# A signal for each tile and another order of TensorE's products in the edge phases of a four-layer graph network kernel

## Time and profile before

| what | value |
|---|---|
| median of 3 runs | 2502.88 us (2497.65 to 2503.34) |
| the profiled execution's own time | 2481.36 us |
| its span | 2479.6 us |
| mean granted clock of TensorE | 0.76 of full speed |
| first edge phase | about 284 to 945 us of the span |
| second edge phase | about 1568 to 2270 us of the span |

### The profile page before, as it was taken

How to read it: one execution, slowest core, us unless ns; L and a number is a source line. 1 busy time by engine, 2 the same in 40 slices (tenths; PEclk the granted TensorE clock), 3 DMA queues, 4 the chain that set the end, 5 groups by cost and what they waited for, 6 DMA issues and landing times. The chain is left out here.

```text
span 2479.6 us, 40282 instructions
## 1 busy us (share of the span) xinstructions
PE 1639.9 (66%) x9301; PEld 1175.0 (47%) x9301; DVE 1690.6 (68%) x4231; ACT 1080.0 (44%) x2994; POOL 1264.8 (51%) x1217
## 2 busy tenths in 40 slices
PE   0678466565666665289999956466676666766378
PEld 0576244343444444289999954233333333333266
DVE  8997766666666667677778646567777777777811
ACT  0474334443333343212222226676676676664321
POOL 0387566666666660126666610655666565652042
PEclk9889667667666666599999977566677667777689
DMA  3014444444444443289999962555665565663331
GB/s 101 2 5 68 152 107 108 109 108 110 109 108 110 107 98 67 65 281 279 301 303 303 305 213 77 172 164 160 167 165 165 161 167 162 167 169 49 91 87 22
DMA packets 212676, 351.09 MB, mean 142 GB/s; under 512 B 45840, under 2 KB 123980, under 8 KB 212588
## 3 DMA queue, kind: packets, MB, share of 16 engines
q0 software_dynamic: 75616, 167.60, 27.1%
q1 hardware_dynamic: 136972, 182.41, 23.9%
HBM read 318.55 MB, written 31.34 MB: 141 GB/s over the span
## 5 line engine op out<-in xcount | busy, mean ns | idle before, releaser
L1164 POOL DMA_INDIRECT e_rows<-table,e_gidx x880 | 846.5, 962 | 525.2 <-issue 233.1
L1227 DVE TENSOR_TENSOR acc<-acc,e_psO 128x260 f32 (+1 forms) x880 | 463.5, 527 | 274.9 <-DMA edge_rows<-row_out 156.6
L1437 PE MATMUL e_psO<-e_rows,e_oh 128*128 128x260 f32 x880 | 374.5, 594 | 233.4 <-DVE acc L1227 206.0
L1437 PEld LDWEIGHTS e_psO<-e_rows,e_oh 128*128 128x128 f32 x880 | 236.3, 290 | 314.6 <-DVE acc L1227 209.3
L2277 PE MATMUL e_psO<-e_rows,e_oh 128*128 128x456 bf16 x440 | 225.1, 512 | 95.3 <-DVE acc L1227 84.1
L1318 PE MATMUL e_psA<-e_own_of_unit,e_ohT 128*128 (+2 forms) x880 | 104.1, 184 | 188.2 <-issue 80.4
L1318 PEld LDWEIGHTS e_psA<-e_own_of_unit,e_ohT 128*128 128x128 bf16 x880 | 82.0, 103 | 274.6 <-issue 263.3
L1406 ACT ACTIVATE e_rows<-e_psA 128x16 f32<-128x16 f32 x110 | 20.3, 184 | 399.5 <-DVE e_psA L1397 300.8
L788 POOL DMA_INDIRECT records<-ordered,s_chunk x68 | 119.1, 1752 | 110.7 <-DVE s_chunk L615 80.9
L2179 ACT ACTIVATE away<-iota_b,etype 128x200 bf16<-128x200 bf16 x440 | 165.3, 446 | 0.0
L2237 DVE TENSOR_SCALAR e_oh<-iota_b,seg,inverse 128x128 bf16<-128x128 bf16 x440 | 117.9, 337 | 69.3 <-issue 57.7
(11 more groups left out here) (444 smaller groups left out, 3669.6 us busy)
## 6 DMA issues: line engine op xcount, KB each, us to landing
hot_run<-in_L_ffn_w_dram SPq DMA_DIRECT2D x107, 512.0 KB
XN<-in_L_ffn_w_dram SPq DMA_DIRECT2D x85, 512.0 KB
e_edge_row<-edge_rows SPq DMA_DIRECT2D x110, 256.0 KB
e_edge_row<-edge_rows SPq DMA_DIRECT2D x110, 128.0 KB
e_rows<-table,e_gidx POOLq DMA_INDIRECT x880
table<-frow SPq DMA_DIRECT2D x25, 192.5 KB
table<-chunk_steps SPq DMA_DIRECT2D x25, 130.0 KB, 2.2
normed_rows<-Z SPq DMA_DIRECT2D x5, 642.5 KB
```

What stands on the lines that cost most here:

```text
L1164: pool.indirect_dma_start(out=rows[:, r, t, 0:width], out_offset=None, in_=table, in_offset=bass.IndirectOffsetOnAxis(ap=gidx[:, r, t:t + ...
L1227: v.tensor_tensor(d, d, psO[:, units * (r % (4 // units)) + j, 0:accw], ALU.add).then_inc(S["added"], 1)
L1437: return pe.matmul(out[:, 0:A0], oh[:, r, t, :], rows[:, r, t, :], start=start, stop=stop)
```

## The change

TensorE's step makes the placing product of group s-1 first and the own product of s+1 after it; the waits ahead of each move along. Each tile's last matmul in a placing product adds one to `summed`, so a group adds four in place of one. GpSimd waits ahead of each of its four gathers for that tile's placing product of four groups ago, with a `hold` each, where it waited once for the group. VectorE waits ahead of each add for that tile's product, and has a `hold` ahead of each add. The other waits for `summed` wait for the same event as before, counted in tiles.

```diff
--- before.py
+++ after.py
@@ -1157,10 +1157,10 @@
                         return
                     g, q, r = at
 
-                    back(pool, S["summed"], g, DEPTH)
                     pool.wait_ge(S["gidx_ready"], g + 1)
-                    hold(pool, "pool")
                     for t in range(TPG):
+                        back(pool, S["summed"], g, DEPTH, per=TPG, extra=t + 1 - TPG)
+                        hold(pool, "pool")
                         pool.indirect_dma_start(
                             out=rows[:, r, t, 0:width], out_offset=None, in_=table,
                             in_offset=bass.IndirectOffsetOnAxis(ap=gidx[:, r, t:t + 1], axis=0))\
@@ -1205,7 +1205,7 @@
                             .then_inc(S["ohT_ready"], 1)
 
                     if l:
-                        back(dve, S["summed"], g, DEPTH)
+                        back(dve, S["summed"], g, DEPTH, per=TPG)
                         hold(dve, "dve")
 
                 def tiles_of(at):
@@ -1218,10 +1218,10 @@
 
                 def add(at, tiles, j):
                     g, q, r = at
-                    if j == 0:
-                        dve.wait_ge(S["summed"], g + 1)
+                    dve.wait_ge(S["summed"], g * TPG + (j + 1) * tpu)
 
                     if not (isinstance(g, int) and g == 0 and j == 0):
+                        hold(dve, "dve")
                         dve.wait_ge(S["added"], g * units + j)
                     d = acc[:, bass.ds(tiles[j], 1), :].rearrange("p a w -> p (a w)")
                     v.tensor_tensor(d, d, psO[:, units * (r % (4 // units)) + j, 0:accw], ALU.add).then_inc(S["added"], 1)
@@ -1302,6 +1302,21 @@
 
                 def step(s, dyn):
                     nxt, last = (locate(s, dyn, d) for d in (1, -1))
+                    if last is not None:
+                        g, q, r = last
+                        pe.wait_ge(S["payload"], g + 1)
+                        if post.get("spread"):
+                            pe.wait_ge(S["weight_kept"], g + 1)
+
+                        pe.wait_ge(S["counted" if l else "oh_ready"], g + 1)
+                        for t in range(TPG):
+                            u = t // tpu
+                            if t % tpu == 0:
+
+                                back(pe, S["added"], g, 4 // units, per=units, extra=u + 1 - units)
+                            ins = post["product"](pe, psO[:, units * (r % (4 // units)) + u, :], oh, rows, r, t,
+                                                  t % tpu == 0, t % tpu == tpu - 1)
+                            ins.then_inc(S["summed"], 1)
                     if nxt is not None:
                         g, q, r = nxt
                         pe.wait_ge(S["ohT_ready"], g + 1)
@@ -1322,21 +1337,6 @@
                                 ins = pe.matmul(out, ohR[0:R - P, r % 2, 1, t, :], relcol[0:R - P, 1, :], start=False,
                                                 stop=True)
                         ins.then_inc(S["own_e"], 1)
-                    if last is not None:
-                        g, q, r = last
-                        pe.wait_ge(S["payload"], g + 1)
-                        if post.get("spread"):
-                            pe.wait_ge(S["weight_kept"], g + 1)
-
-                        pe.wait_ge(S["counted" if l else "oh_ready"], g + 1)
-                        for t in range(TPG):
-                            u = t // tpu
-                            if t % tpu == 0:
-
-                                back(pe, S["added"], g, 4 // units, per=units, extra=u + 1 - units)
-                            ins = post["product"](pe, psO[:, units * (r % (4 // units)) + u, :], oh, rows, r, t,
-                                                  t % tpu == 0, t % tpu == tpu - 1)
-                        ins.then_inc(S["summed"], 1)
                 pipeline(pe, 1, 1, step, post.get("pe_besides", ()))
 
         end_phase()
@@ -1421,7 +1421,7 @@
                 ins.then_inc(spaced, 1)
 
                 if not isinstance(g, int) or g >= DEPTH:
-                    act.wait_ge(S["summed"], g - (DEPTH - 1))
+                    act.wait_ge(S["summed"], (g - (DEPTH - 1)) * TPG)
                 act.wait_ge(spaced, g + 1)
                 nc.scalar.activation(oh[:, r, :, :], apart[:, :, :], ACT.Relu, scale=-1.0, bias=ones[:, 0:1])\
                     .then_inc(S["oh_ready"], 1)
@@ -2180,7 +2180,7 @@
                                                bias=etype1[:, bass.ds(g * TPG + t, 1)])
                 ins.then_inc(measured, 1)
 
-                back(act, S["summed"], g, DEPTH)
+                back(act, S["summed"], g, DEPTH, per=TPG)
                 act.wait_ge(measured, g + 1)
                 nc.scalar.activation(counts[:, :, T1:T1 + R], away[:, :, :], ACT.Relu, scale=-1.0, bias=ones[:, 0:1])\
                     .then_inc(S["counted"], 1)
```

## The result

The change made the kernel slower: 2632.93 us (median of 4 runs, 2623.94 to 2641.56) against 2502.74 (4 runs), ratio 1.0525, 95% interval 1.0486 to 1.0563. The profiled execution took 2623.94 us, its span is 2622.2, against 2481.36 and 2479.6 before.

The account below looks back on a forecast made before the run. Waits in the ring of groups, not busy time, were taken to bound the kernel. First phase 0, second phase 11 us and shortened starts 1 us gave -12: 2502.88 - 12 = 2491 us, range 2450 to 2550.

Parts of the forecast that it names:

- What bounds the kernel: Ring of groups in both edge phases: waits bound it, not busy time; product signals late in a gather run await its drain.
- Part 1: TensorE's signal for each tile, 660 more increments in all: taken as 0, upper bound 152 us.
- The estimate of 17 us: TensorE's 660 added increments at 0.026 us each, by the skill page's rule; no profile row showed it.
- Parts 2 and 3: Added waits and holds for each tile, on VectorE ahead of adds and GpSimd ahead of gathers: each taken as 0.
- The upper ends (72 and 99): Highest costs allowed for added waits and holds: 72 us a phase on VectorE, 99 us on GpSimd.
- Part 4: TensorE's placing product ahead of the own product: VectorE's add 0.7 us later in one of two steps, hidden; 39 us uncovered.
- rival D: Own product's signal, behind the placing product, delays VectorE's reduce: 2536 to 2594 us, likeliest 2536; chance 0.19.
- The gain in the sum: Second phase: gather runs of four become eight, 11 us, plus 1 us for shortened group starts: -12 us.
- A: The forecast: gather runs of four turn into eight, -5 to -25 us; chance 0.37.
- The 1 us for shortened starts: Gain of 1 us added to the sum for the shortened group starts.
- rival B: No change: the drain releases held signals whatever their tile, VectorE's gain is waited away at the next; 2503 us, chance 0.16.

Follow-up runs that it names:

- the tile parts alone: Signals, waits and holds of each tile in both phases, TensorE's order as in the kernel before: 2522.35 us against 2501.17, ratio 1.0095.

## Why the prediction was wrong

Forecast 2491 us, range 2450 to 2550; measured 2632.93. The sign was wrong and the range too narrow by 83 us. By its steps:

- **What bounds the kernel.** Right for the kernel before on such a chip: gathers in runs, and TensorE's late signals seen only behind them. It was also true that the last to end ahead of a resuming GpSimd is a late `summed`. What it did not say is that this is a property or a state of the chip, which the trace of one chip can't show. The rule read from it, that signals up to some point in a run pass and later ones wait for the drain, did not carry over to phase 2 or to the whole change (3.86 us passed and was held; 0.76 us was seen 2.15 us late, in the middle of the run).
- **Part 1, increments at 0.** Right as far as seen: ratio 0.9997 on the chip without holds, with an interval that holds no change. The estimate of 17 us from the page "TensorE: Matmul & The Clock Gate" of the Trainium skill, section "The cost: per-tile semaphore tail" (whose tiles are small matmuls packed side by side), did not show there: the interval of the ratio ends at 1.0011, which is 2.4 us. On a chip with holds the increments were not run alone.
- **Parts 2 and 3, waits at 0.** Right for each by itself in phase 1 (686.5 and 680.3), wrong for both together: 31 to 36 us. The upper ends (72 and 99) held it.
- **Part 4 is the step that failed.** I priced the later own product at 0.7 us "in one of two steps", hidden by the run, so at nothing. With the order alone that is what phase 1 showed. In phase 2 it cost 170 us on its own (882.8 us against 713.8 and 711.0 with the old order), because VectorE's reduce waited for the own signal up to 7.3 us at a time and everything behind it waited too. The working was done on the first phase's rows; the second's came only into rival D.
- **The gain in the sum did not come either.** Runs of four did not become runs of eight. With the tile parts alone 600 us of phase 2 (1640 to 2240) have 50 + 25 waits of GpSimd for others, where the earlier trace rows had 63 waits, and the phase took 711.0 and 713.8 us. So the forecast, A, was wrong without the new order too. In the same 600 us 92 adds waited 97.4 us under "issue": what VectorE gains at a tile it waits for at the next, which was rival B's sentence. The 1 us for shortened starts in the sum has no row.
- **Rival D was the mechanism,** with its place (the reduce behind the own product), its sign (65 such waits in 600 us, 2.4 us each) and the phase that it hits most. I gave it 0.19. Its reason, a point between 3.8 and 4.9 us up to which signals pass, is not what the rows show. In the whole change runs of the second phase carry one group, as it said, but a group costs 787.3 / 110 = 7.2 us and not 6.66, so the phase lost 88 us and not 33; the first lost 62, and D had 58 for it only as its far end. With the order alone it was another pattern: a run kept its eight gathers, because both products that release them were done, but the next product could start only after the drain, and its time then lay bare in the pause: 16.7 us for eight, where I had put 13.3. A held signal ahead of a chain costs the length of the chain, not only the hold. "GpSimd could start again on the first tile of the late product" was right too, and worth 63 us.

## What to carry to other kernels

Where an engine releases another through a short product, give that signal first: the order "small product that the other side waits for, then the long one" was worth 170 us here against its reverse, on chips where TensorE's signals are seen late during gathers. When one instruction is moved behind another, follow its signal to every waiting engine, and price the whole chain behind it as if it ran alone. Splitting one handover into four gained nothing here by itself: each of the four signals can be late.

## What was not expected of the hardware

- The same kernel took 2226 us on one chip and 2500 to 2506 on five occasions on others. On the first, signals of TensorE were seen within 0.03 us among running gathers; on the others, with gathers issued at the same 1.25 us, own products were seen late, most often only behind the run, with waits of up to 7.3 us in the second phase. Where in the run they ended does not tell which: 3.86 us passed in one phase and was held in the other.
- Neither fewer bytes in the gathers (a half and a fifth) nor a wider spacing (1.47 us) ended the holding.
- Two kinds of waits that were free each by itself cost 31 to 36 us together.
